# Expert tiles as two 64-row halves in half columns of the array, two tiles per step

## The chip, the cores and the metric

The kernel runs on one core of one Trainium2 chip. The metric is the device time in microseconds (us); lower is better. A core has TensorE for matrix products (PE in the profile, its weight loads PEld), VectorE (DVE), ScalarE (ACT), GpSimd (POOL) and SyncE (SP).
## The reference, cut to what matters

One layer over 4096 tokens of width D = 256: an attention part with fast weights, then a mixture of experts (E = 64 experts, TOP_K = 6 for each token, hidden width F = 176), then a shared expert and a weighted sum.

```python
scores = jax.nn.softmax(x @ gate_w.T, axis=-1)
topk_w, topk_idx = jax.lax.top_k(scores, TOP_K)        # 6 of 64 experts for each token
...
buf = zeros((E, C, D)).at[se, pos_c].add(x[st])         # rows sorted by expert, C = 768 at most
g = jnp.einsum('ecd,efd->ecf', buf, w_gate)
u = jnp.einsum('ecd,efd->ecf', buf, w_up)
eo = jnp.einsum('ecf,edf->ecd', jax.nn.silu(g) * u, w_down)
gathered = eo[se, pos_c] * (sw * valid)[:, None]
y = jnp.zeros_like(x).at[st].add(gathered)
```

There are 4096 x 6 = 24576 (token, expert) rows, 384 for an expert in the mean; how many each expert has is known only on the chip. Everything in the expert stage is float32.

## The kernel before

Five phases follow each other, with all engines meeting between them: `phase_qkv`, `phase_fast_weights` (which also normalises, picks the experts and scatters each row to its expert's stretch of `scratch_buf`), `phase_route`, `phase_experts` and `phase_combine`.

`phase_route` counts the rows of each expert and makes tables for the expert tiles: for tile n the first row in `scratch_buf` (`first_row`), the expert (`need`, as its number plus one), and which of the tile's rows are real (`slot`, `beyond`). A tile is 128 rows of one expert. The number of tiles is fixed when the kernel is built, by the worst case: (24576 + 64 x 127) / 128, rounded up to a multiple of 128, is NT = 256. Meanwhile POOL scatters the last rows (L1603) and SP loads the first four experts.

`phase_experts` runs 256 steps, all unrolled, on every engine in an order written out by hand. For tile n:

- ACT's sequencer loads `first_row[n]` into a register (`load_x`, L1779) and issues the DMA of 128 rows into `xg` (L1781), some six tiles ahead;
- PE turns the tile (`turn_x`, L1721, two 128x128 transposes into `psX`), ACT copies it to `xT` (L1791);
- PE multiplies it with the gate and up weights (`gate_up`, L1735, `psGU`, 352 columns, two products of depth 128). The weights lie in a ring of eight experts; which slot is read from `need[n]` by PE's sequencer (`expert_of`, L1725). ACT makes the silu (`sgm`, L1787), DVE the product (`hh`, L1868);
- PE turns `hh` (`turn_h`, L1743 and L1744, `psH`), DVE copies it to `hT` (L1846);
- PE makes the down product (`down`, L1751, `psD`, 256 columns, two products of depth 88), ACT copies it to `eo` (L1798), POOL scatters the rows to `scratch_y` (L1709) at places that DVE worked out (L1851, L1871).

One step of PE is `gate_up(n-1), turn_x(n), turn_h(n-2), down(n-3)`; one of ACT is silu(n-1), copy of x(n), copy of the output(n-3), `load_x(n+6)`. DVE also makes the tokens' weights in these steps (L1821 to L1862). SP refills the ring as experts are done with (`freed`). `phase_combine` gathers, weighs and adds.

In `phase_fast_weights` there is a product that the later text uses: `token_product` (L764), whose stationary operands are 64 columns wide and whose outputs lie in the upper and the lower 64 partitions of PSUM by turns:

```python
for h in range(H):
    for b2 in range(2):
        mm = pe.matmul(dst[CH * b2:CH * b2 + CH, h * HD:(h + 1) * HD],
                       kvT[:, x, j0 + h, b2, :], src[:, 2 * b2 + h, :], start=True, stop=True)
```

Of the kernel before, what the change touches and what calls it, by code (L numbers as in the profile page):

```python
# [6 lines left out]
F32 = mybir.dt.float32  # L7
# [23 lines left out]
NT = -(-((N * TOPK + E * (P - 1)) // P) // P) * P  # L31
WRING = 8
FIRST = 4
# [1352 lines left out]
def load_expert(sp, T, wgu, wd, ex, buf, done):  # L1386
    FH = F // 2
    for c, key in enumerate(("wgT", "wuT")):
        sp.dma_start(wgu[:, bass.ds(buf, 1), :, c * F:(c + 1) * F].rearrange("p b k n -> p (b k) n"),
                     T[key].rearrange("e (k p) n -> e p k n", p=P)  # L1390
                     [bass.ds(ex, 1), :, :, :].rearrange("e p k n -> (e p) k n")).then_inc(done, 16)
    sp.dma_start(wd[0:FH, bass.ds(buf, 1), :, :].rearrange("p b k n -> p (b k) n"),
                 T["wdT"].rearrange("e (k p) n -> e p k n", p=FH)
                 [bass.ds(ex, 1), :, :, :].rearrange("e p k n -> (e p) k n")).then_inc(done, 16)

def phase_route(nc, T, z, mask, run, ones, low, valid, slot, beyond, need, first_row, freed, wgu, wd, rows, dest):

    TC = NT // P  # L1400
    HP = E // 2
    with ExitStack() as ctx:
# [10 lines left out]
        identb = sb("identb", [P, P], BF16)  # L1413
# [4 lines left out]
        lane = sb("lane", [P, 2])  # L1418
        total = sb("total", [P, E])
        end = sb("end", [P, 2 * E])  # L1420
        ended = sb("ended", [P, 3, TC, E])
        col = sb("col", [P, 4, TC])
        left = sb("left", [P, TC])
        back = sb("back", [P, TC])
        cols = sb("cols", [P, 4 * TC, P], BF16)
        row = sb("row", [P, 3, NT])
# [6 lines left out]
        psT = ctx.enter_context(nc.psum_tensor("t_psT", [P, 2, NT], F32))  # L1433
        psL = ctx.enter_context(nc.psum_tensor("t_psL", [P, 2, NT], F32))
# [8 lines left out]
        def _(v):  # L1443
# [25 lines left out]
            v.wait_ge(s_pool, 9)  # L1469
# [3 lines left out]
            for c in range(TC):  # L1473
# [3 lines left out]
                                            op0=ALU.is_le, op1=ALU.mult, accum_out=col[:, 1, c:c + 1]))  # L1477
# [4 lines left out]
            step(v.tensor_tensor(col[:, 1, :], tcol[:, :], col[:, 1, :], ALU.subtract))  # L1482
            settle()
            step(v.scalar_tensor_tensor(out=left[:, :], in0=col[:, 1, :], scalar=-float(P), in1=left[:, :], op0=ALU.mult, op1=ALU.add))
            settle()
            step(v.tensor_scalar(left[:, :], left[:, :], 0.0, float(P), ALU.max, ALU.min))
            step(v.tensor_scalar(back[:, :], col[:, 1, :], 1.0, None, ALU.min))
            settle()
            step(v.tensor_scalar(col[:, 2, :], left[:, :], -1.0, float(P), ALU.mult, ALU.add))
            settle()  # L1490
            step(v.tensor_tensor(col[:, 2, :], col[:, 2, :], back[:, :], ALU.mult))
            settle()
            step(v.tensor_tensor(col[:, 3, :], col[:, 2, :], left[:, :], ALU.add))
            settle()
            step(v.tensor_copy(cols[:, :, :], col[:, :, :].rearrange("p a c -> p (a c)").unsqueeze(2).broadcast_to([P, 4 * TC, P])), "cols")
            step(v.tensor_scalar(freed[:, WRING:E], end[0:1, 0:E - WRING], float(TILES_AHEAD), None, ALU.add))
# [4 lines left out]
            v.wait_ge(s_row, 1)  # L1501
            step(v.tensor_scalar(row[:, 0, :], psT[:, 0, :], float(STRETCH), None, ALU.mult))
            step(v.tensor_scalar(need[:, :], psT[0:1, 0, :], float(E - 1), 1.0, ALU.min, ALU.add))
            settle()
            step(v.scalar_tensor_tensor(out=row[:, 1, :], in0=psT[:, 1, :], scalar=float(P), in1=row[:, 0, :],
                                        op0=ALU.mult, op1=ALU.add))
            v.wait_ge(s_left, 1)
            settle()
            step(v.tensor_tensor(row[:, 2, :], row[:, 1, :], psL[:, 0, :], ALU.subtract))
            settle()  # L1510
            step(v.tensor_scalar(first_row[:, :], row[0:1, 2, :], float(E * STRETCH), None, ALU.min))
            step(v.tensor_scalar(slot[:, :], row[:, 2, :], float(E * STRETCH), lane[:, 1:2], ALU.min, ALU.add))
# [6 lines left out]
            step(v.tensor_scalar(outside[:, 0, :], psL[:, 0, :], lane[:, 0:1], BIG, ALU.is_gt, ALU.mult))  # L1519
            step(v.tensor_scalar(outside[:, 1, :], psL[:, 1, :], lane[:, 0:1], BIG, ALU.is_le, ALU.mult))  # L1520
# [14 lines left out]
        @block.sync  # L1535
        def _(sp):
            for ex in range(FIRST):
                load_expert(sp, T, wgu, wd, ex, ex, s_w)
            sp.wait_ge(s_w, 48 * FIRST)

        @block.tensor
        def _(pe):
            pe.matmul(psN[0:E, 0:1], run[:, TT, :], ones[:, 0:1], start=True, stop=True)
            pe.matmul(psN[:, P:P + E], ones[:, :], run[:, TT, :], start=True, stop=True).then_inc(s_count, 1)
            pe.wait_ge(s_pool, 9)
# [3 lines left out]
            for a in range(2):  # L1549
                for c in range(TC):  # L1550
                    mm = pe.matmul(psT[:, a, c * P:(c + 1) * P], cols[:, a * TC + c, :], identb[:, :], start=True, stop=True)
            mm.then_inc(s_row, 1)
            for a in range(2):
                for c in range(TC):
                    mm = pe.matmul(psL[:, a, c * P:(c + 1) * P], cols[:, (2 + a) * TC + c, :], identb[:, :], start=True, stop=True)
            mm.then_inc(s_left, 1)
# [13 lines left out]
        def _(pool):  # L1570
# [4 lines left out]
            pool.memset(identb[:, :], 0.0).then_inc(s_pool, 1)  # L1575
            pool.wait_ge(s_pool, 4)
# [4 lines left out]
            pool.affine_select(out=identb[:, :], in_=identb[:, :], compare_op=ALU.not_equal, fill=1.0, base=0,  # L1581
                               pattern=[[-1, P]], channel_multiplier=1).then_inc(s_pool, 1)
            pool.iota(tcol[:, :], pattern=[[P, TC]], base=0, channel_multiplier=1,
# [5 lines left out]
            pool.wait_ge(s_pool, 11)  # L1589
# [18 lines left out]
def phase_experts(nc, T, ident, slot, beyond, need, first_row, freed, p, mask, valid, key, keys, wk, wgu, wd, wsh, wdn, xh):  # L1608
# [5 lines left out]
    TI = 8  # L1614
# [3 lines left out]
    XA = GB - 2  # L1618
    WEIGHTS = 28
    with ExitStack() as ctx:  # L1620
# [20 lines left out]
        picked = sb("picked", [P, 2, E])  # L1641
        psX = ps("psX", [P, 2, 512])
# [15 lines left out]
        def thru(n):  # L1658
            return TILES_AHEAD + 1 + n

        def steps(eng, step, after):

            for n in range(NT + after):
# [461 lines left out]
```

## Time and profile before

| what | value |
|---|---|
| time, median of 3 runs | 1771.67 us (1770.18 to 1774.84) |
| the profiled execution's own time | 1769.68 us |
| its span, first to last instruction | 1767.3 us |
| PE busy over the span | 90% |
| DVE, ACT, POOL busy | 65%, 50%, 46% |
| mean granted TensorE clock | 0.964 of full |
| expert steps, 971 to 1617 us | PE busy 643.61 of 646.00 us |

The profiled execution takes 2.4 us more than its span, and is 2.0 us below the median of the runs. Shares of busy time are means over phases with different limits; the stage that the change touches has to be read by itself. A row of a timeline merges equal instructions (x4) and gives the start of the first and the time to the end of the last. Matrix products are pipelined: one shows from its first input to its last output, so that the next starts well before it ends.

### The profile page before, as it was taken

Reading aid. Unit: us, or ns where it says so; the run is one execution under the profiler, and the core shown is the slowest. Engines: PE = TensorE matmul, PEld = TensorE weight load, DVE = VectorE, ACT = ScalarE, POOL = GpSimd, SP = SyncE. Lnnn points to the kernel's source line nnn. Section 1 sums busy time; section 2 is a strip of 40 time slices with the busy share of each in tenths; the row PEclk is TensorE's granted clock in tenths of the full one; section 3 lists DMA queues with packets and bytes.
Section 4 is the critical chain, followed back from the end, with each engine's and each line's share of the span. In section 5 each row is a group of like instructions: output and inputs, shape, how many; then the busy total and the mean of one; then the engine's idle time right before and its main releaser. Section 6 shows DMA issues by size and latency. Waiting matters only on the chain. (4 is left out here: it accounts for less than half of the span.)

```text
span 1767.3 us, 40874 instructions
## 1 busy us (share of the span) xinstructions
PE 1591.9 (90%) x11235; PEld 1184.7 (67%) x11235; DVE 1147.2 (65%) x4093; ACT 880.9 (50%) x2156; POOL 817.9 (46%) x882
## 2 busy tenths in 40 slices
PE   7995999888889888988862999999999999998997
PEld 4664667666666666666652677777777777776775
DVE  5664878788888788888864554444444444433887
ACT  4773767666666666666641333333333333332221
POOL 2322334566566566666675233333333343343333
PEclk9996999999999999999965999999999999999998
DMA  3864444444444532232224656556555656322996
GB/s 131 258 226 153 129 143 128 156 134 141 152 150 153 163 95 83 83 89 83 74 89 135 183 175 186 172 171 185 171 175 176 182 179 194 98 54 62 252 245 152
DMA packets 260031, 263.27 MB, mean 149 GB/s; under 512 B 83563, under 2 KB 231385, under 8 KB 259824
## 3 DMA queue, kind: packets, MB, share of 16 engines
q1 hardware_dynamic: 196016, 170.45, 33.4%
q0 software_dynamic: 21504, 51.18, 8.2%
q10 hardware_dynamic: 42304, 39.08, 8.1%
q8 instruction: 105, 1.72, 0.4%
q14 instruction: 102, 0.84, 0.2%
HBM read 141.78 MB, written 127.18 MB: 152 GB/s over the span
## 5 line engine op out<-in xcount | busy, mean ns | idle before, releaser
L1709 POOL DMA_INDIRECT scratch_y<-e_eo,e_goes x256 | 251.7, 983 | 405.3 <-ACT e_eo L1798 336.6
L1735 PE MATMUL e_psGU<-wgu,e_xT 128*128 x1024 | 352.1, 466 | 3.1 <-issue 2.3
L1846 DVE COPY e_hT<-e_psH 88x256 f32<-88x256 f32 x256 | 107.7, 421 | 338.6 <-PE e_psH L1744 242.2
L1751 PE MATMUL e_psD<-wd,e_hT 88*128 x1024 | 263.6, 379 | 0.0
L1735 PEld LDWEIGHTS e_psGU<-wgu,e_xT 128*128 128x128 f32 x1024 | 186.7, 190 | 87.6 <-issue 18.3
L1369 POOL TENSOR_TENSOR f_wnr<-f_wss,f_half 128x4 f32<-128x4 f32 x96 | 109.3, 1139 | 230.7 <-DVE f_wss L1192 230.1
L1359 POOL DMA_INDIRECT scratch_buf<-rows,dest x180 | 185.3, 1030 | 45.5 <-issue 43.7
L1787 ACT ACTIVATE e_sgm<-e_psGU 128x176 f32<-128x176 f32 x256 | 81.2, 317 | 238.5 <-PE e_psGU L1735 206.6
L1751 PEld LDWEIGHTS e_psD<-wd,e_hT 88*128 88x128 f32 x1024 | 173.8, 190 | 14.3 <-issue 0.3
L1798 ACT ACTIVATE e_eo<-e_psD 128x256 f32<-128x256 f32 x256 | 98.1, 383 | 161.8 <-issue 87.6
L1721 PEld LDWEIGHTS e_psX<-ident,e_xg 128*128 128x128 f32 x512 | 72.4, 142 | 76.7 <-issue 40.8
L1721 PE MATMUL e_psX<-ident,e_xg 128*128 128x128 f32 x512 | 98.6, 274 | 9.0 <-DMA e_xg<-scratch_buf 9.0
L1011 ACT ACTIVATE f_wsq<-f_WT 128x512 f32<-128x512 f32 x96 | 60.6, 631 | 74.3 <-DVE f_WT L1188 68.9
L1791 ACT ACTIVATE e_xT<-e_psX 128x256 f32<-128x256 f32 x256 | 97.2, 380 | 0.4
L856 PEld LDWEIGHTS prod<-f_A 128*128 128x128 bf16 x768 | 59.8, 99 | 46.6 <-issue 2.2
L979 ACT ACTIVATE f_X<-spare 128x512 bf16<-128x512 f32 x96 | 57.4, 598 | 65.8 <-PE spare L873 65.8
L284 PE MATMUL q_psQ<-q_wq,q_hT 128*128 128x512 f32 (+1 forms) x256 | 90.2, 496 | 0.0
L1868 DVE TENSOR_TENSOR e_hh<-e_psGU,e_sgm 128x176 f32<-128x176 f32 x256 | 84.9, 332 | 3.6 <-ACT e_sgm L1787 3.6
L2025 DVE SCALAR_TENSOR_TENSOR c_acc<-c_g,wk,c_acc 128x256 f32<-128x256 f32 x160 | 78.6, 491 | 5.7
L853 PE MATMUL prod<-f_gamma_r,f_gamma_l 128*128 128x512 bf16 x192 | 74.7, 389 | 7.0 <-DVE f_A L1179 6.4
L856 PE MATMUL prod<-f_A 128*128 128x128 bf16 x768 | 75.1, 221 | 0.0
L979 ACT ACTIVATE f_B<-prod 128x512 bf16<-128x512 f32 x96 | 57.0, 595 | 35.6 <-PE prod L856 22.6
(303 smaller groups left out, 3773.2 us busy)
## 6 DMA issues: line engine op xcount, KB each, us to landing
e_xg<-scratch_buf ACTq DMA_DIRECT2D x256, 132.0 KB
scratch_y<-f_blank SPq DMA_DIRECT2D x64, 384.0 KB
c_g<-scratch_y SPq DMA_DIRECT2D x64, 384.0 KB, 6.1
scratch_qkvT<-q_tT SPq DMA_DIRECT2D x16, 768.0 KB, 5.1
wgu<-in_wgT SPq DMA_DIRECT2D x64, 176.0 KB
wgu<-in_wuT SPq DMA_DIRECT2D x64, 176.0 KB
wd<-in_wdT SPq DMA_DIRECT2D x64, 176.0 KB
scratch_buf<-f_blank SPq DMA_DIRECT2D x65, 132.0 KB, 1.9
```

Source lines behind the costliest of these rows:

```text
L284: mm = pe.matmul(psQ[:, u, lo:hi], hT[:, b % 2, k, u, :], wq[:, k, lo:hi], start=(k == 0), stop=(k == KD - 1))
L856: mm = pe.matmul(dst[:, q, :], a[:, x, m, q, :], a[:, x, m, q, :], start=False, stop=(q == Q - 1))
L979: act.activation(dst, src, ACT.Copy, scale=scale).then_inc(done.sem, 1)
L1359: pool.indirect_dma_start(out=T["buf"], out_offset=bass.IndirectOffsetOnAxis(dest[:, i, k:k + 1], 0), in_=rows[:, i % RR, :], in_offset=No ...
L1369: pool.tensor_tensor(wnr[:, x, cols], wss[:, x, cols], half[:, 0:Q], ALU.pow).then_inc(wn1[x].sem, 1)
L1709: pool.indirect_dma_start(out=T["y"], out_offset=bass.IndirectOffsetOnAxis(goes[:, n:n + 1], 0), in_=eo[:, n % OB, :], in_offset=None, bou ...
L1721: mm = pe.transpose(psX[:, j % 2, k * P:(k + 1) * P], xg[j % GB][:, k * P:(k + 1) * P], ident[:, :])
L1735: mm = pe.matmul(psGU[:, j % 2, 0:2 * F], xT[:, j % 2, k, :], wgu[:, bass.ds(buf, 1), k, :].rearrange("p b n -> p (b n)"), start=(k == 0), ...
L1751: mm = pe.matmul(psD[:, j % 2, 0:D], hT[0:FH, j % 2, k, :], wd[0:FH, buf, k, :].rearrange("p b n -> p (b n)"), start=(k == 0), stop=(k == 1))
L1791: act.activation(xT[:, j % 2, :, :].rearrange("p k t -> p (k t)"), psX[:, j % 2, 0:KD * P], ACT.Copy).then_inc(xd, 1)
L1798: act.activation(eo[:, b % OB, :], psD[:, b % 2, 0:D], ACT.Copy).then_inc(eod, 1)
L1846: v.tensor_copy(hT[0:FH, b, :, :].rearrange("p k t -> p (k t)"), psH[0:FH, b, 0:2 * P]).then_inc(htd, 1)
```

## The change

An expert tile becomes two halves of 64 rows, each with a first row and an expert of its own (mostly the same one, at a border two). NT becomes (24576 + 64 x 63) / 64, halved and rounded up to a multiple of 8: 224. The two halves share the tile's 128 partitions. `turn_x` and `turn_h` stay whole; the products of `gate_up` and `down` are split into one of 64 stationary columns for each half, side by side in the array: the first half reads its weights from the ring at an address known only at run time, the second from a copy, `up2` and `down2`, that ACT (`keep_up`, 128x704) and DVE (`keep_down`, 88x512) make for each tile. `load_x` issues two DMAs of 64 rows. Every engine works on two tiles in a step, and the register values of two tiles (four entries of a table) are loaded by one call, `numbers`, without a check of bounds. POOL waits for an expert's weights (`has_come`, one register load for each tile) and tells ACT. `phase_route` makes tables of half tiles: other small DVE work, seven smaller products in place of eight for the tables (their number of columns is much the same), one identity less on POOL.

```diff
-NT = -(-((N * TOPK + E * (P - 1)) // P) // P) * P
+RT = P // 2
+NT = -(-((N * TOPK + E * (RT - 1)) // RT) // 16) * 8
...
+        def numbers(engine, table, lo, hi, n):
+            _, values = nc.values_load_multi_w_load_instructions(
+                table[0:1, 2 * n:2 * n + 4], [engine], min_val=lo, max_val=hi, skip_runtime_bounds_check_because=IN_RANGE)
+            return {n + i // 2: values[i // 2 * 2:i // 2 * 2 + 2] for i in (0, 2)}
...
         def _(pool):
+            def has_come(m):
+                pool.wait_ge(ready, pool.value_load(need[0:1, 2 * m + 1:2 * m + 2], min_val=1, max_val=E))
+                pool.sem_inc(present, 1)
...
         def _(pe):
+            def find(n):
+                for m, (e1, _) in numbers(mybir.EngineType.PE, need, 1, E, n).items():
+                    at[m] = pe.snap((e1 + (NB - 1)) % NB * WROW)
-            def gate_up(n, j, expert):
-                e1, buf = expert
-                pe.wait_ge(ready, e1)
+            def gate_up(n):
+                pe.wait_ge(up_kept, n + 1)
                 pe.wait_ge(xd, thru(n))
                 pe.wait_ge(hd, thru(n - 2))
                 for k in range(KD):
-                    mm = pe.matmul(psGU[:, j % 2, 0:2 * F], xT[:, j % 2, k, :],
-                                   wgu[:, bass.ds(buf, 1), k, :].rearrange("p b n -> p (b n)"),
+                    pe.matmul(psGU[0:RT, n % 2, 0:2 * F], xT[:, n % 2, k, 0:RT], ring[:, bass.ds(at[n] + k * 2 * F, 2 * F)],
+                              start=(k == 0), stop=(k == KD - 1))
+                    mm = pe.matmul(psGU[RT:P, n % 2, 0:2 * F], xT[:, n % 2, k, RT:P], up2[:, n % 2, k * 2 * F:(k + 1) * 2 * F],
                                    start=(k == 0), stop=(k == KD - 1))
...
+                pe.wait_ge(down_kept, n + 1)
                 for k in range(2):
+                    pe.matmul(psD[0:RT, n % 2, 0:D], hT[0:FH, n % 2, k, 0:RT], ring[0:FH, bass.ds(at[n] + UP + k * D, D)],
+                              start=(k == 0), stop=(k == 1))
+                    mm = pe.matmul(psD[RT:P, n % 2, 0:D], hT[0:FH, n % 2, k, RT:P], down2[:, n % 2, k * D:(k + 1) * D],
+                                   start=(k == 0), stop=(k == 1))
...
+            for n in range(-2, NT + 2, 2):
+                each(gate_up, n)
+                each(down, n - 2)
+                each(turn_x, n + 2)
+                if 0 <= n + 2 < NT:
+                    find(n + 2)
+                each(turn_h, n)
...
         def _(act):
+            def load_x(m):
+                if m >= GB:
+                    act.wait_ge(xp, thru(m - GB))
+                    act.wait_ge(goes_d, m - GB + 1)
+                act.sem_inc(a_carrier, 1)
+                for h, at in enumerate(rows.pop(m)):
+                    act.dma_start(xg[m % GB][h * RT:(h + 1) * RT, :], T["buf"][bass.ds(at, RT), :]).then_inc(gi[m % GB], 16)
+            def keep_up(n):
+                e1 = experts.pop(n)[1]
+                act.wait_ge(present, n + 1)
+                act.wait_ge(gup, thru(n - 2))
+                act.sem_inc(a_carrier, 1)
+                act.activation(up2[:, n % 2, :], ring[:, bass.ds((e1 + (NB - 1)) % NB * WROW, UP)], ACT.Copy).then_inc(up_kept, 1)
...
+            for n in (0, 2):
+                find_rows(n)
+                load_x(n)
+                load_x(n + 1)
+            act.preload_act_table_set("silu_and_others")
+            find_experts(0)
+            keep_up(0)
+            keep_up(1)
+            for n in range(-2, NT + 2, 2):
+                (find_rows(n + 6), find_experts(n + 2), silu(n), keep_up(n + 2), load_x(n + 6), silu(n + 1),
+                 keep_up(n + 3), keep_out(n - 2), load_x(n + 7), keep_x(n + 2), keep_x(n + 3), keep_out(n - 1))
...
         def _(v):
+            def keep_down(n):
+                v.wait_ge(up_kept, n + 1)
+                v.wait_ge(dp, thru(n - 2))
+                at = (experts.pop(n)[1] + (NB - 1)) % NB * WROW + UP
+                v.tensor_copy(down2[:, n % 2, :], ring[0:FH, bass.ds(at, 2 * D)]).then_inc(down_kept, 1)
+            for n in range(0, NT + 2, 2):
+                (keep_h(n - 2), keep_h(n - 1), own(n), weigh(n), own(n + 1), weigh(n + 1), hidden(n), leave(n),
+                 hidden(n + 1), leave(n + 1), numbers(DVE, need, n), keep_down(n), keep_down(n + 1))
```

The loops of ACT and DVE are written here in one line each, without the conditions for the first and the last tiles. `find_rows` and `find_experts` are `numbers` on `first_row` and `need`. `keep_x`, `keep_out`, `keep_h`, `own`, `hidden`, `leave` are the old work on L1791, L1798, L1846, L1851, L1868 and L1871 under names.

## Rows read from the trace of the kernel before

**Rows 1.** The page: busy us, share of the span and instructions of each engine.

```profile
PE 1591.9 (90%) x11235; PEld 1184.7 (67%) x11235; DVE 1147.2 (65%) x4093; ACT 880.9 (50%) x2156; POOL 817.9 (46%) x882
```

**Rows 2.** Windows: end of route, expert steps, drain, combine.

```profile
930.00:971.00 41.00, 10.23 (x56) 7.07 (x56) 20.16 (x98) 5.75 (x7) 23.41 (x39) 0.54 0.41 131
971.00:1617.00 646.00, 643.61 (x3054) 478.21 (x3055) 305.22 (x1677) 248.62 (x763) 247.75 (x252) 0.99 0.54 159
1617.00:1627.00 10.00, 5.24 (x21) 3.23 (x19) 1.42 (x6) 1.47 (x4) 3.94 (x4) 0.90 0.05 8
```

**Rows 3.** Timeline of one steady expert step: start, us, engine, line, idle before.

```profile
1613.47 1.35 PE L1735 MATMUL e_psGU<-wgu,e_xT 128*128 x4
1614.66 0.38 PE L1721 MATMUL e_psX<-ident,e_xg 128*128 128x128 f32 x2
1614.86 0.32 ACT L1787 ACTIVATE e_sgm<-e_psGU 128x176 f32<-128x176 f32 x1 [0.80 <-PE e_psGU L1735]
1614.88 0.27 PE L1743 MATMUL e_psH<-ident,e_hh 128*88 128x128 f32 x1
1615.09 1.03 PE L1751 MATMUL e_psD<-wd,e_hT 88*128 x4
1615.96 1.35 PE L1735 MATMUL e_psGU<-wgu,e_xT 128*128 x4
```

**Rows 4.** Timeline of ACT alone over one step of the expert stage.

```profile
1303.90 0.32 ACT L1787 ACTIVATE e_sgm<-e_psGU 128x176 f32<-128x176 f32 x1 [0.85 <-PE e_psGU L1735]
1304.11 0.38 ACT L1791 ACTIVATE e_xT<-e_psX 128x256 f32<-128x256 f32 x1
1305.18 0.38 ACT L1798 ACTIVATE e_eo<-e_psD 128x256 f32<-128x256 f32 x1 [0.69 <-issue]
1306.24 0.36 ACTq L1781 DMA_DIRECT2D e_xg<-scratch_buf  x1
1306.64 0.32 ACT L1787 ACTIVATE e_sgm<-e_psGU 128x176 f32<-128x176 f32 x1 [1.08 <-PE e_psGU L1735]
```

**Rows 5.** Timeline of PE around one `token_product` (L764).

```profile
408.38 0.66 PE L901 MATMUL prod<-ident,f_WT 128*128 128x128 f32 x4 [0.77 <-DVE f_WT L1205]
408.96 0.66 PE L764 MATMUL prod<-f_Wn,f_kvT 128*64 128x128 f32 x8
409.55 0.66 PE L964 MATMUL spare<-wgate,f_h2T 128*128 128x64 f32 x4
```

**Rows 6.** Lines L1779 and L1781, 1100 to 1500 us: ns, min/median/max.

```profile
L1779 ACTq TENSOR_LOAD <-first_row x159: 276/349/566, 1100.7 to 1498.2; - x159
L1779 ACTq FUSED_REGOPS  x159: 152/152/158, 1101.2 to 1498.5; - x159
L1781 ACTq FUSED_REGOPS  x159: 42/42/42, 1101.5 to 1498.8; - x159
L1781 ACTq MOVE e_xg<-scratch_buf x159: 29/29/38, 1101.6 to 1498.9; - x159
L1781 ACTq DMA_DIRECT2D e_xg<-scratch_buf x159: 353/358/430, 1101.6 to 1499.2; - x159
```

**Rows 7.** Groups of instructions with 512 columns, as the nearest to the new copies.

```profile
L1011 ACT ACTIVATE f_wsq<-f_WT x96: 621/630/664, 177.2 to 896.0; 128x512 f32<-128x512 f32 x96
L1188 DVE TENSOR_TENSOR f_WT<-prod,f_WT 128x512 f32<-128x512 f32 x3 | 2.1, 689 | 2.2 <-PE prod L890 2.2
```

**Rows 8.** Timeline where the expert steps begin.

```profile
967.32 1.54 ACTq L1781 DMA_DIRECT2D e_xg<-scratch_buf  x2
970.29 0.38 ACT L1791 ACTIVATE e_xT<-e_psX 128x256 f32<-128x256 f32 x1
970.95 2.71 PE L1735 MATMUL e_psGU<-wgu,e_xT 128*128 x4 [0.70 <-ACT e_xT L1791]
978.57 2.11 PE L1735 MATMUL e_psGU<-wgu,e_xT 128*128 x4 [0.24 <-issue]
```

**Rows 9.** Timeline of the last scatter and of the combine's first product.

```profile
1622.37 0.98 POOL L1709 DMA_INDIRECT scratch_y<-e_eo,e_goes  x1 [0.30 <-issue]
1625.60 2.69 PE L1950 MATMUL c_psG<-wsh,xh 128*128 128x352 f32 x4 [4.72 <-PEq L67]
```

**Rows 10.** Route: POOL's group of scatters, and the last work of DVE.

```profile
L1603 POOL DMA_INDIRECT scratch_buf<-rows,dest x12 | 11.9, 988 | 3.5 <-issue 3.5
963.77 1.45 DVE L1525 TENSOR_SCALAR valid<-t_psV 128x512 bf16<-128x512 f32 x2 [4.28 <-DMA f_qT<-scratch_qkvT]
```

More of the change, by code:

```diff
@@ L29 @@
 TT = N // P
-NT = -(-((N * TOPK + E * (P - 1)) // P) // P) * P
+RT = P // 2
+NT = -(-((N * TOPK + E * (RT - 1)) // RT) // 16) * 8
 WRING = 8
+UP = 2 * F * KD
+WROW = UP + 2 * D
+IN_RANGE = "route clips the table's entries to these bounds"
 FIRST = 4
@@ L1500, in _ @@
                 settle()
[L1501 to L1512, printed above, removed]
             for g in range(NG):
@@ L1617, in phase_experts @@
     OB = 4
-    XA = GB - 2
+    SEEN = 6
     WEIGHTS = 28
@@ L1753, in down @@
                 mm.then_inc(dp, 1)
-            def step(n, j):
-                if real(n, 1):
-                    up = expert_of(n - 1)
-                    gate_up(n - 1, (j - 1) % TI, up)
-                if real(n, 3):
-                    out_of = expert_of(n - 3)
-                if real(n, 0):
-                    turn_x(n, j)
-                if real(n, 2):
-                    turn_h(n - 2, (j - 2) % TI)
-                if real(n, 3):
-                    down(n - 3, (j - 3) % TI, out_of)
@@ L1768, in _, with each @@
-            steps(pe, step, 3)
+                del at[n]
+            def each(stage, n):
+                for m in (n, n + 1):
+                    if 0 <= m < NT:
+                        stage(m)
+            for n in range(-2, NT + 2, 2):
[5 more added lines that the diff above has]
+                each(turn_h, n)
         @block.scalar
@@ L1773, in _, with silu, keep_x, keep_out @@
                 act.sem_inc(s, TILES_AHEAD)
+            def silu(n):
+                act.wait_ge(gup, thru(n))
+                act.activation(sgm[:, n % 2, :], psGU[:, n % 2, 0:F], ACT.Silu).then_inc(sgd, 1)
+            def keep_x(n):
+                act.wait_ge(xp, thru(n))
+                act.wait_ge(gup, thru(n - 2))
+                act.activation(xT[:, n % 2, :, :].rearrange("p k t -> p (k t)"), psX[:, n % 2, 0:KD * P],
+                               ACT.Copy).then_inc(xd, 1)
+            def keep_out(n):
+                act.wait_ge(dp, thru(n))
+                if n >= OB:
+                    act.wait_ge(out[n % OB], n // OB * 16)
+                act.activation(eo[:, n % OB, :], psD[:, n % 2, 0:D], ACT.Copy).then_inc(eod, 1)
+            rows, experts = {}, {}
+            def find_rows(n):
+                rows.update(numbers(mybir.EngineType.Activation, first_row, 0, E * STRETCH, n))
+            def find_experts(n):
+                experts.update(numbers(mybir.EngineType.Activation, need, 1, E, n))
             def load_x(m):
@@ new lines, in _ @@
+            for n in (0, 2):
[7 more added lines that the diff above has]
+            for n in range(-2, NT + 2, 2):
+                if real(n, -6):
+                    find_rows(n + 6)
+                if 2 <= n + 2 < NT:
+                    find_experts(n + 2)
+                if real(n, 0):
+                    silu(n)
+                    if real(n, -2):
+                        keep_up(n + 2)
+                if real(n, -6):
+                    load_x(n + 6)
+                if real(n, 0):
+                    silu(n + 1)
+                    if real(n, -2):
+                        keep_up(n + 3)
+                if real(n, 2):
+                    keep_out(n - 2)
+                if real(n, -6):
+                    load_x(n + 7)
+                if real(n, -2):
+                    keep_x(n + 2)
+                    keep_x(n + 3)
+                if real(n, 2):
+                    keep_out(n - 1)
```

257 lines of the change are left out of this document (136 added, 121 removed).

## The prediction

> **What bounds the kernel now.** I read the page's busy shares first: PE leads with 90%, but that is a mean over five phases [rows 1]. So I cut the span into windows by phase. In the expert steps PE is busy 643.61 of 646.00 us, DVE 305 us, ACT 249 us, POOL 248 us [rows 2]: the stage is bound by PE alone, and the others have 1.3 to 1.5 us free in each step. One steady step of the timeline says what PE does in it: from one `gate_up` to the next are 1615.96 - 1613.47 = 2.49 us [rows 3]. Of these `gate_up` takes 1.19 (to the start of `turn_x`), `turn_x` and `turn_h` 0.43 together, `down` 0.87 (1615.09 to 1615.96). There is no gap, so a step is the sum of what PE streams, and ACT, whose silu starts 0.03 to 0.05 us after `gate_up` ends, is on no path as long as it keeps up.
>
> The whole stage: the first `gate_up` starts at 970.95 [rows 8], the last, 255 steps later, at 1615.96 [rows 3]: 645.0 us, 2.529 a step. 255 steps of 2.487 would be 634.2; of the other 10.8 about 2.7 are the start, where two steps take 7.62 us at a low clock [rows 8], and 8.1, or 0.032 a step, are steps in which something is late. Rows 4 show what: a register load and a DMA issue end just when the silu starts (1306.24 + 0.36 = 1306.60, silu at 1306.64). ACT's sequencer is close behind PE.
>
> **What goes: 32 of 256 steps.** The rest of the change decides what a step costs. If it cost nothing, 32 x 2.52 = 81 us would go.
>
> **PE's products.** There are as many columns to stream as before, if the two halves run side by side, and twice as many if not. The trace has such products: `token_product` makes four float32 products of 64 stationary columns, 128 moving, in alternating halves, as eight records. In the full array a record of 128 columns takes 0.107 (`gate_up`: 1.19 / 4 = 0.298 for 352 columns, so 0.108 for 128). Eight would take 0.86, but the next line starts 0.59 after L764 [rows 5]: they run in pairs, 4 x 0.107 = 0.43. What is left over is the price of going in and out of half columns: the last record of L901 starts at 408.38 + 0.66 - 0.27 = 408.77, L964 at 409.55; 0.78 less its own 0.107 and less 0.43 is 0.24 us. An iteration of two tiles goes in and out once. So PE needs 2 x 2.487 + 0.24 = 5.21 us for two tiles, 2.61 a step. Bounds: 2.49 (the price of the switch vanishes) and, with no pairing at all, 2 x (1.19 + 0.87) + 0.43 + 0.12 = 4.67; I take the pairing, for the row is the same kind of product, only narrower.
>
> **PE's register loads** fall from two a step to one for two tiles, and before they hid behind queued products; I count nothing. If that cover goes, one load of 0.35 and its arithmetic of 0.15 stand in the open in an iteration, 0.25 a step.
>
> **ACT.** New are `keep_up` (704 columns; 512 take 0.630 [rows 7], 176 take 0.32 and 256 take 0.38 [rows 4], so 0.83 ns a column and 0.79 us), a second DMA for each tile (0.358 + 0.042 + 0.029 = 0.43 us of its sequencer [rows 6]) and loads of four values in place of one. I lay this out with T = 0 where `gate_up(n)` starts. silu(n) starts at T+1.4, `keep_up(n+2)` runs to 2.45, hiding one pair of DMA issues; silu(n+1) waits for PE until 2.57, `keep_up(n+3)` runs to 3.65, the output copy to 4.0, two DMA issues to 4.5. PE's `turn_x(n+2)` is done at 2.38 + 1.74 + 0.12 + 0.22 + 0.17 = 4.63, so the copy of x runs 4.65 to 5.03, and `gate_up(n+2)` could start at 5.07 where PE comes to it at 5.21. Then ACT copies x(n+3) and output(n-1), and its sequencer is free at about 5.4. The next silu is due at 5.21 + 1.4 = 6.6. In between stand `find_rows` and `find_experts`: 1.2 us of room, and with 0.15 of slack at the silus and 0.15 at the copy of x, 1.5 us. They cost two loads and some 0.3 of address arithmetic. If a load of four values takes what a load of one takes, 0.349 and 0.152 [rows 6], it is 1.3 us: it fits, barely. No row shows a load of several values: its bounds are 0.35 and four times that, 1.4. I take the low end, since it is one call with neighbouring values and the check that costs arithmetic today is gone; the high end is a rival.
>
> **DVE** is busy 1.19 a step [rows 2]; `keep_down` adds at most 0.69 [rows 7] and a load 0.25, so 2.1 of 2.61: hidden. Its copy of `hT(n)` comes behind both `keep_down`, at about T+5.9, and `down(n)` wants it at 5.21 + 2.4 = 7.6. **POOL**: 0.98 for a scatter and about 0.55 for `has_come`, 1.5 of 2.61; hidden. If the weights of a tile six ahead were late, POOL would hold back scatters and ACT `keep_up`; SP refills eight experts ahead, so I count nothing.
>
> **The ends.** Before, the first DMA issue is at 967.32 and the first copy of x at 970.29 [rows 8]. Now twelve DMA issues (5.2 us), four register loads (1.6) and part of two `keep_up` (1.6) stand before that copy: about 8 us instead of 3, +5. Filling and draining in pairs: +1 each; before, the last scatter starts 6.4 us after the last `gate_up`, and combine's first product 3.2 us later [rows 9]. Together +7, between +3 and +11. In route POOL's twelve scatters, 0.99 each with 0.3 between [rows 10], and not the tables, fill the time; they can start 0.5 earlier, DVE has some more small steps: 0, give or take 1.5.
>
> **Sum.** From the first to the last `gate_up`: 223 x (2.605 + 0.032) + 2.7 = 590.8 against 645.0: -54.2. With the ends -47.2. The profiled execution's own time, 1769.68, becomes 1722.5; the median of the runs is 2.0 above it: 1724.5.
>
> **The rivals.** *ACT is late because of its register loads; it decides from 0.81 us a load* (slower). The excess over PE's iteration is 2 x load + 0.3 - 1.5. The gain is used up when a step takes (645.0 - 7 - 2.7) / 223 - 0.032 = 2.817, an iteration 5.63, an excess of 0.42, a load of 0.81. At four times 0.349 = 1.4 the excess is 1.6: 5.21 + 1.6 = 6.8, 3.4 a step, 223 x 3.44 + 2.7 = 770, so about 1769.7 + 125 + 7 + 2 = 1904. For it speaks that ACT has only 0.2 us to spare; against it that all four values lie side by side. Chance 0.19.
>
> *The same in between*: a load of 0.70, the geometric middle of the bounds, gives an excess of 0.2, a step of 2.71, 223 x 2.74 + 2.7 = 613.7: -31 + 7, so about 1747. Chance 0.17, with 0.06 more for a time within 0.3% of before. The Trainium skill (Runtime: NRT & Kernel Launch, Instruction fetch mechanics) says that register loads cost about 200 ns for each register, in bulk too. By an estimate from that page four registers are 0.8 us, the excess 0.4, and the time would be about that of before. This trace has 0.35 us for one register; no row has several.
>
> *The halves don't pair* at 352 columns or with an address known only at run time: 4.67 a step, 223 x 4.7 = 1048, some 2180 us. Rows 5 speak against it; chance 0.03. That the switch costs nothing, with ends of +3, gives 223 x 2.52 + 2.7 = 564.7, -80 + 3: 1695; chance 0.05.
>
> **Numbers.** The forecast itself, 1700 to 1742, has 0.50; its own range takes loads up to 0.6 us, ends of +3 to +11, a switch of 0.1 to 0.3. Adding the middle rival and the slower one up to about 1 us a load gives 1700 to 1805 for 8 in 10. Faster 0.72, same 0.06, slower 0.22; 0.3% of the time, 5.3 us, is about what a measurement tells from no change.
>
> **What would show it.** In the profile after: 224 tiles; `gate_up` records in pairs, an iteration near 5.2 us; about 0.1 us of PE idle before the first half product and before `turn_x`; `up2` copies of 0.79 us; a four-value load of 0.35 to 0.4 us on ACTq. If PE waits for ACT's copy of x and ACT's silu starts later than 0.05 us after `gate_up` ends, with register loads ahead of it, the rival has it. The first copy of x should come about 5 us later than before. I am wrong if PE's busy time in the stage falls while its span doesn't, or if pairs are absent.

## The result, and the profile after

The changed kernel takes 1788.2 us (median of 4 runs, 1781.58 to 1794.65) against 1770.93 for the kernel before (4 runs, 1767.56 to 1774.84): ratio 1.0092, 95% interval 1.0064 to 1.0121. It is 0.9% slower, where 1724.5 us was forecast. The profiled execution, the fastest of the four, took 1781.58 us, its span is 1779.7.

The page's busy shares answer to [rows 1], the window of the expert steps to [rows 2]:

```profile
PE 1549.5 (87%) x12655; PEld 1056.7 (59%) x12655; DVE 1219.9 (69%) x4177; ACT 999.9 (56%) x2284; POOL 788.9 (44%) x848
```

```profile
976.00:1622.00 646.00, 592.79 (x4424) 345.53 (x4424) 372.02 (x1731) 365.53 (x888) 217.47 (x219) 1.00 0.52 151
```

PE was busy 643.61 of 646.00 us in the expert steps; now it is busy 592.79 of 646.00. It does 51 us less work in the same time: the saving is there, and has turned into 53 us of idle. The page's groups say in front of what it waits:

```profile
L1769 PE MATMUL e_psGU<-wexp,e_xT 128*64 x896 | 290.2, 467 | 57.7 <-issue 52.5
L1771 PE MATMUL e_psGU<-e_up,e_xT 128*64 128x352 f32 x896 | 290.7, 468 | 0.0
```

Behind the first bar stand the busy time (us) and the mean of one (ns), behind the second PE's idle time before them. It is all in front of `gate_up`'s first half product. "issue" names nobody, so one iteration (two tiles) has to be read. The timeline from one `gate_up` of a pair to the next, PE, ACT and ACT's queue; columns as in [rows 3]:

```profile
1341.05 0.32 ACT L1813 ACTIVATE e_sgm<-e_psGU 128x176 f32<-128x176 f32 x1 [1.15 <-PE e_psGU L1771]
1341.29 0.79 ACT L1848 ACTIVATE e_up<-wexp 128x704 f32 x1
...
1341.53 1.14 ACTq L1841 DMA_DIRECT2D e_xg<-scratch_buf  x2
...
1341.72 0.46 PE L1769 MATMUL e_psGU<-wexp,e_xT 128*64 x1
...
1341.73 0.46 PE L1771 MATMUL e_psGU<-e_up,e_xT 128*64 128x352 f32 x1
...
1342.72 0.32 ACT L1813 ACTIVATE e_sgm<-e_psGU 128x176 f32<-128x176 f32 x1 [0.64 <-PE e_psGU L1771]
...
1342.98 0.79 ACT L1848 ACTIVATE e_up<-wexp 128x704 f32 x1
...
1343.32 0.49 ACTq L1841 DMA_DIRECT2D e_xg<-scratch_buf  x1
...
1343.54 0.38 PE L1788 MATMUL e_psD<-e_down,e_hT 88*64 88x256 f32 x1
...
1343.85 0.66 PE L1761 MATMUL e_psX<-ident,e_xg 128*128 128x128 f32 x4
1343.96 0.49 ACTq L1841 DMA_DIRECT2D e_xg<-scratch_buf  x1
...
1344.56 0.66 ACT L1818 ACTIVATE e_xT<-e_psX 128x256 f32<-128x256 f32 x2 [0.51 <-PE e_psX L1761]
...
1345.20 0.51 PE L1769 MATMUL e_psGU<-wexp,e_xT 128*64 x1 [0.26 <-issue]
```

Read it backwards. `gate_up` starts at 1345.20, 0.26 us after the first copy of x has ended (1344.56 + 0.38; the row's 0.66 is that of two copies). That copy starts right behind the second DMA issue of a pair (1343.96 + 0.49 = 1344.45), not behind `turn_x`. This pair is late because silu(n+1) started at 1342.72 and not at 1342.25, when its products had ended (1341.73 + 0.46 is 1342.19); what ended just before it is the other pair of issues (1341.53 + 1.14 = 1342.67). The same kernel, 40 us earlier, where one issue takes 0.91:

```profile
1301.79 0.91 ACTq L1841 DMA_DIRECT2D e_xg<-scratch_buf  x1
1302.15 0.37 ACT L1825 ACTIVATE e_eo<-e_psD 128x256 f32<-128x256 f32 x1
1302.86 0.50 ACTq L1841 DMA_DIRECT2D e_xg<-scratch_buf  x1
1303.46 0.66 ACT L1818 ACTIVATE e_xT<-e_psX 128x256 f32<-128x256 f32 x2 [0.94 <-PE e_psX L1761]
...
1304.10 0.51 PE L1769 MATMUL e_psGU<-wexp,e_xT 128*64 x1 [0.69 <-issue]
```

Here the copy of x is held up by 0.4 us more, and the gap in front of `gate_up` is 0.69 in place of 0.26: what ACT's queue holds ahead of that copy reaches PE in full. The source rows, 1100 to 1500 us, price the steps of ACT and DVE (ns, min/median/max, as [rows 6]):

```profile
L1687 ACTq TENSOR_LOAD <-first_row x68: 305/309/322, 1105.2 to 1495.7; - x68
L1687 ACTq TENSOR_LOAD <-need x68: 304/306/325, 1105.5 to 1496.0; - x68
...
L1841 ACTq DMA_DIRECT2D e_xg<-scratch_buf x274: 480/491/1278, 1101.2 to 1498.7; - x137
...
L1848 ACT ACTIVATE e_up<-wexp x138: 789/790/792, 1100.9 to 1499.5; 128x704 f32 x138
...
L1955 DVE COPY e_down<-wexp x136: 415/423/425, 1103.5 to 1495.1; 88x512 f32 x136
```

The four-value load, which decided between forecast and slower rival, is 0.31 us, cheaper than the load of one value before. The DMA issue, taken from [rows 6] as 0.358, is 0.491: it moves 64 rows now and not 128. Of all 448 issues 41 take over 0.56 us (these I call long); none of the 256 before took over 0.43. They do not come just anywhere: 31 are the second of a pair, 10 the third issue of an iteration, 0.65 us behind the first pair; the first of an iteration, 2.7 us behind the one before it, is never long.

From the start of the first `gate_up` (976.68) to that of the last iteration (1622.07) are 645.4 us, 111 iterations of 5.814. The median iteration, from the starts of `gate_up` in the trace, is 5.62; a quarter take more than 5.97. The 38 iterations with a long issue in them take 6.10 in the mean, the other 73 take 5.67.

The ends. Where the expert steps begin and where they end (answers to [rows 8] and [rows 9]):

```profile
966.44 5.57 ACTq L1841 DMA_DIRECT2D e_xg<-scratch_buf  x8
...
976.68 0.84 PE L1769 MATMUL e_psGU<-wexp,e_xT 128*64 x1 [5.14 <-ACT e_xT L1818]
```

```profile
1633.46 0.98 POOL L1743 DMA_INDIRECT scratch_y<-e_eo,e_goes  x1 [2.55 <-issue]
```

The first `gate_up` comes 5.7 us later than before. The last tile's `gate_up` is at 1623.30, combine's first product at 1636.70, 13.4 us later; before it was 9.6. The span adds up: last tile's `gate_up` minus first 646.6 against 645.0 (+1.6), start +5.7, drain +3.8, after that +1.3: 12.4 us, which is 1779.7 - 1767.3.

### The profile page after: what moved, and what is told of

Same layout as the page of the kernel before. It is cut to its first block and busy times, and to the rows that moved or that the text cites. A ratio compares the mean times of both kernels' runs of the same rounds, so it can differ in the third digit from the quotient of the medians.

```text
span 1779.7 us, 43893 instructions
## 1 busy us (share of the span) xinstructions
PE 1549.5 (87%) x12655; PEld 1056.7 (59%) x12655; DVE 1219.9 (69%) x4177; ACT 999.9 (56%) x2284; POOL 788.9 (44%) x848
## 5 line engine op out<-in xcount | busy, mean ns | idle before, releaser
L1769 PE MATMUL e_psGU<-wexp,e_xT 128*64 x896 | 290.2, 467 | 57.7 <-issue 52.5
L1771 PE MATMUL e_psGU<-e_up,e_xT 128*64 128x352 f32 x896 | 290.7, 468 | 0.0
L1769 PEld LDWEIGHTS e_psGU<-wexp,e_xT 128*64 128x64 f32 x896 | 114.0, 137 | 185.9 <-issue 87.9
L1786 PE MATMUL e_psD<-wexp,e_hT 88*64 x896 | 211.9, 379 | 0.6 <-DVE e_hT L1917 0.6
L1788 PE MATMUL e_psD<-e_down,e_hT 88*64 88x256 f32 x896 | 211.9, 379 | 0.0
L1848 ACT ACTIVATE e_up<-wexp 128x704 f32 x224 | 176.9, 790 | 0.2 <-issue 0.2
L1786 PEld LDWEIGHTS e_psD<-wexp,e_hT 88*64 88x64 f32 x896 | 122.2, 136 | 79.3 <-issue 0.9
L1788 PEld LDWEIGHTS e_psD<-e_down,e_hT 88*64 88x64 f32 x896 | 122.2, 136 | 0.0
L1771 PEld LDWEIGHTS e_psGU<-e_up,e_xT 128*64 128x64 f32 x896 | 114.0, 137 | 0.0
L1955 DVE COPY e_down<-wexp 88x512 f32 x224 | 93.0, 423 | 22.9 <-PE e_psD L1788 2.5
```

The source lines that it names most:

```text
L1769: pe.matmul(psGU[0:RT, n % 2, 0:2 * F], xT[:, n % 2, k, 0:RT], ring[:, bass.ds(at[n] + k * 2 * F, 2 * F)], start=(k == 0), stop=(k == KD - 1))
L1771: mm = pe.matmul(psGU[RT:P, n % 2, 0:2 * F], xT[:, n % 2, k, RT:P], up2[:, n % 2, k * 2 * F:(k + 1) * 2 * F], start=(k == 0), stop=(k == K ...
L1786: pe.matmul(psD[0:RT, n % 2, 0:D], hT[0:FH, n % 2, k, 0:RT], ring[0:FH, bass.ds(at[n] + UP + k * D, D)], start=(k == 0), stop=(k == 1))
L1788: mm = pe.matmul(psD[RT:P, n % 2, 0:D], hT[0:FH, n % 2, k, RT:P], down2[:, n % 2, k * D:(k + 1) * D], start=(k == 0), stop=(k == 1))
L1848: act.activation(up2[:, n % 2, :], ring[:, bass.ds((e1 + (NB - 1)) % NB * WROW, UP)], ACT.Copy).then_inc(up_kept, 1)
L1955: v.tensor_copy(down2[:, n % 2, :], ring[0:FH, bass.ds(at, 2 * D)]).then_inc(down_kept, 1)
```

## The experiments

Kernel n below is that of experiment n; what the expectations call e1 to e6 are kernels 1 to 6. An iteration is two tiles. The theories, as the expectations name them: **A**, ACT is late for its copy of x because of what its queue holds (issues, copies of weights); **B**, PE itself pays, for the half columns; **C**, DVE is late; **D**, the long issues come at random and cannot be arranged away. The experiments ran on three chips, on which the kernel before takes 1732.48, 1782.35 and 1733.44 us, so a time is compared only with kernels on its own chip; between chips I compare iterations (first to last start of `gate_up` over 111, and the median). If nothing changes, an iteration is the changed kernel's: 5.81 in the mean, 5.62 in the median.

**1. The copy of 704 columns and its load go from ACT to DVE.**

```diff
-            def keep_up(n):                      # ACT
-                act.activation(up2[:, n % 2, :], ring[...], ACT.Copy).then_inc(up_kept, 1)
+            def keep_up(n):                      # DVE
+                v.tensor_copy(up2[:, n % 2, :], ring[...]).then_inc(up_kept, 1)
```

> The 128x704 copies of the up weights and their register load move from ACT to DVE; results unchanged. Theory A (ACT is the late engine: its DMA issues of 0.49 us and its copies of 0.79 us stand before silu and before the copy of x that gate_up waits for): an iteration of two tiles falls from 5.81 to about 5.3 us, the time to 1730 to 1745 us, some 50 us under the changed kernel and 30 under the one before. Theory B (half columns, run-time addresses and PE's own waits make the iteration 5.6 to 5.8): no change, 1780 to 1795. Theory C (DVE becomes the late engine, 2.2 us of 2.6 a tile): above 1790.

1731.43 us (10 runs) against 1732.48 for before (13 runs): ratio 0.9996 (0.9986 to 1.0005). The iteration is 5.71, median 5.59. Taking 1.6 us of copies and a load from ACT gives only 0.1 us back; the 5.3 of theory A is missed. 36 issues are long, up to 1.73 us. If ACT is late, it is not mainly for its copies. DVE has 1.03 us more to do in an iteration and nothing gets slower, so C is out.

**2. After the first eight tiles only one DMA for each tile** (the other 64 rows are old ones and are not scattered).

```diff
-                for h, at in enumerate(rows.pop(m)):
+                for h, at in enumerate(rows.pop(m)[0:2 if m < GB else 1]):
```

> Only the first 64 rows of each tile are loaded (after the first eight tiles); the second half keeps old rows and is not scattered: one DMA issue for each tile in place of two, all else as in the changed kernel. Theory A: 2 x 0.56 us less of ACT's sequencer in an iteration, which falls to 5.3 to 5.4 us, the time to about 1740. Theory B: 5.8 us, 1780 or more. If ACT's copies alone make it late and not the issues: 5.7.

1695.75 us (one run), 36.7 less than before on that chip; iteration 5.370, median 5.36. All work of PE, both copies and all loads are still there; every second issue is gone, with the rows that it would bring and their scatter (kernel 5 has these back at the same median, so that traffic is not what counts). ACT's timeline:

```profile
1302.82 0.32 ACT L1814 ACTIVATE e_sgm<-e_psGU 128x176 f32<-128x176 f32 x1 [1.15 <-PE e_psGU L1772]
1303.07 0.79 ACT L1849 ACTIVATE e_up<-wexp 128x704 f32 x1
1303.32 0.48 ACTq L1842 DMA_DIRECT2D e_xg<-scratch_buf  x1
1304.01 0.32 ACT L1814 ACTIVATE e_sgm<-e_psGU 128x176 f32<-128x176 f32 x1
...
1305.10 0.49 ACTq L1842 DMA_DIRECT2D e_xg<-scratch_buf  x1
1306.10 0.66 ACT L1819 ACTIVATE e_xT<-e_psX 128x256 f32<-128x256 f32 x2 [0.78 <-PE e_psX L1762]
```

silu(n+1) is 1.19 us behind silu(n), as PE's products are, where it was 1.67 behind; the copy of x has 0.5 us of free queue ahead of it. And the long issues are gone, though no issue became shorter as such (source rows, 1000 to 1550 us):

```profile
L1842 ACTq DMA_DIRECT2D e_xg<-scratch_buf x197: 481/490/519, 999.7 to 1524.8; - x197
```

**3. ACT's copy cut to 8 of 704 columns** (the second halves use fixed weights), both issues kept.

```diff
-                act.activation(up2[:, n % 2, :], ring[:, bass.ds(..., UP)], ACT.Copy).then_inc(up_kept, 1)
+                act.activation(up2[:, n % 2, 0:8], ring[:, bass.ds(..., 8)], ACT.Copy).then_inc(up_kept, 1)
```

> ACT's copy of the up weights is cut to 128x8 (both buffers are filled once before; the second half computes with those weights), the two DMA issues and all loads and waits stay. Theory A: the copies hide the first pair of issues, so that without them the issues alone are left: silu(n+1) some 0.3 us late in place of 0.5, an iteration of about 5.4 us, 1745. If the issues alone matter: 5.8. Theory B: 5.8.

1751.17 us (one run); 5.821, median 5.63: no change. The copies of 0.79 us are hidden behind the issues (A had them share the blame, and 5.4 expected). In this kernel's timeline, in an iteration with a long issue, the copy of x sits right behind a pair of 1.43 us:

```profile
1305.19 1.43 ACTq L1842 DMA_DIRECT2D e_xg<-scratch_buf  x2
1306.73 0.66 ACT L1819 ACTIVATE e_xT<-e_psX 128x256 f32<-128x256 f32 x2 [1.40 <-PE e_psX L1762]
```

**4. The kernel before, with two DMAs of 64 rows for each tile** and nothing else of the change.

```diff
-                act.dma_start(xg[m % GB][:, :], T["buf"][bass.ds(at, P), :]).then_inc(gi[m % GB], 16)
+                for h in range(2):
+                    act.dma_start(xg[m % GB][h * CH:(h + 1) * CH, :], T["buf"][bass.ds(at + h * CH, CH), :]).then_inc(gi[m % GB], 16)
```

> The kernel before, with each tile of 128 rows loaded by two DMAs of 64 rows; results unchanged. It prices the second issue alone. If a 64-row issue takes 0.49 us as in the changed kernel, ACT's sequencer needs 1.12 us in place of 0.43 where it has no room: a step goes from 2.53 to about 3.1 us, the time to 1890 to 1930. If it takes 0.36, as the prediction had it: 2.9 us, about 1870. Theory B: no change, 1771.

1823.6 us (one run) against 1732.48: 91 us more, 2.871 a step where it was 2.529. Two issues, 1.17 us where one was 0.36, end right before a silu, which PE is then waiting for:

```profile
1302.61 1.17 ACTq L1782 DMA_DIRECT2D e_xg<-scratch_buf  x2
1303.82 0.32 ACT L1788 ACTIVATE e_sgm<-e_psGU 128x176 f32<-128x176 f32 x1 [1.60 <-PE e_psX L1721]
```

The direction is A's, the size six tenths of what was expected (0.34 us a step for 0.57): of 0.8 us more in the queue 0.34 reach PE. It also shows that halves cost 0.48 each without anything else of the change (source rows, 1000 to 1550 us):

```profile
L1782 ACTq DMA_DIRECT2D e_xg<-scratch_buf x386: 479/484/1239, 1000.0 to 1548.4; - x193
```

**5 and 6. The four issues of an iteration one by one**, before silu(n), before silu(n+1), before the output copy and before the copy of x; with the copy of 704 columns on DVE (5) and on ACT (6). **7.** The changed kernel once more on that chip.

```diff
-                if real(n, -6):
-                    load_x(n + 6)
+                if ahead:
+                    load_half(n + 6, 1)
                 if real(n, 0):
                     silu(n + 1)
...
+                if ahead:
+                    load_half(n + 7, 0)
                 if real(n, 2):
                     keep_out(n - 2)
-                if real(n, -6):
-                    load_x(n + 7)
+                if ahead:
+                    load_half(n + 7, 1)
```

> As e1 (copies of the up weights on DVE), and on ACT the four DMA issues of an iteration are spread one by one: before silu(n), before silu(n+1), before the output copy, before the copies of x. Theory A, sharpened by the first four runs (what counts is which 0.49 us issues stand back to back before silu(n+1) and before the copy of x; the copies don't count): an iteration of about 5.4 us with hardly any scatter, against 5.71 in e1 and 5.81 in the changed kernel; a ratio of 0.98 to the kernel before. Rival D (an issue is sometimes long, 0.8 to 1.3 us, whatever stands around it, and the mean comes from those): the usual iteration falls to 5.4, but the mean stays above 5.6, a ratio of 0.99 to 1.0.

> The changed kernel with the four DMA issues spread alone, the copies left on ACT. Both register loads and an issue then stand between the last output copy and silu(n), 1.4 us in 1.5 us of room. Theory A: 5.4 to 5.6 us an iteration, a ratio to the kernel before of 0.98 to 1.0. If the order doesn't matter: 5.8 and 1.009 as the changed kernel.

> The changed kernel itself, on the chip of these runs, to be compared with them and with the kernel before. Both theories: a ratio to the kernel before near 1.009, 5.8 us an iteration.

| kernel | time, us (runs) | ratio to before (95%) | iteration: mean, median |
|---|---|---|---|
| before | 1782.35 (10) | | |
| changed | 1796.6 (7) | 1.0086 (1.0058 to 1.0114) | 5.822, 5.61 |
| 5: spread, copy on DVE | 1751.69 (4) | 0.9814 (0.9766 to 0.9861) | 5.405, 5.36 |
| 6: spread, copy on ACT | 1759.44 (4) | 0.9875 (0.9831 to 0.9918) | 5.534, 5.46 |

Kernel 5 issues as many DMAs as the changed one and computes the same, and is 45 us faster than it; 0.417 an iteration over 111 iterations is 46. It beats the kernel before by 1.9% (1.4 to 2.3). ACT's timeline:

```profile
1299.26 0.32 ACT L1813 ACTIVATE e_sgm<-e_psGU 128x176 f32<-128x176 f32 x1 [1.15 <-PE e_psGU L1771]
1299.48 0.48 ACTq L1837 DMA_DIRECT2D e_xg<-scratch_buf  x1
1300.44 0.32 ACT L1813 ACTIVATE e_sgm<-e_psGU 128x176 f32<-128x176 f32 x1 [0.87 <-PE e_psGU L1771]
1300.67 0.49 ACTq L1837 DMA_DIRECT2D e_xg<-scratch_buf  x1
1301.31 0.38 ACT L1825 ACTIVATE e_eo<-e_psD 128x256 f32<-128x256 f32 x1 [0.55 <-DVE e_goes L1936]
1301.54 0.48 ACTq L1837 DMA_DIRECT2D e_xg<-scratch_buf  x1
1302.54 0.66 ACT L1818 ACTIVATE e_xT<-e_psX 128x256 f32<-128x256 f32 x2 [0.84 <-PE e_psX L1761]
```

No two issues touch, and only 15 of 448 are long, where the changed kernel has 41 and kernel 1, in pairs, 36. So D does not hold: spreading removes most of them, and they do not come at random. In all traces with issues of 64 rows the longest pause before a long issue is 1.09 us (kernel 6); of 1433 issues with more than 1.15 us of pause before them none is long. Closeness alone is not all of it either: in kernel 4 only 11 of 251 second ones of a pair are long, in the changed kernel 31 of 224. Kernel 6 says that the two copies and their register load on ACT matter once the pairs are gone: 0.13 us an iteration; which of the two it is was not told apart. Nine iterations of kernel 5 are over 5.45: the first, 6.65, is the start of the stage (6.65 in kernel 2 as well), seven have a long issue of 0.77 to 1.45 us in them, and one of 6.36 stays open.

The traces also say where the time is lost. Medians over the iterations but the first and last five, from the starts of the instructions, in us:

| kernel | `gate_up` to `turn_x` | `turn_x` to first copy of x (mean) | end of the copy to `gate_up` | silu(n+1) behind silu(n) |
|---|---|---|---|---|
| changed | 4.25 | 0.73 (0.93) | 0.26 | 1.67 |
| 1 | 4.25 | 0.71 (0.82) | 0.26 | 1.40 |
| 2 | 4.25 | 0.47 (0.47) | 0.26 | 1.18 |
| 3 | 4.25 | 0.74 (0.94) | 0.26 | 1.67 |
| 5 | 4.25 | 0.47 (0.50) | 0.26 | 1.18 |

Only the stretch from `turn_x` to the copy differs: 4.25 + 0.47 + 0.38 + 0.26 is 5.36, and with 0.93 in place of 0.47 it is 5.82. Kernel 1 adds that the late silu(n+1) is not needed for it: there it is only 0.2 late, and the pair of issues behind the output copy is enough to hold the copy of x back by 0.24.

**8. Three more four-value loads in each iteration of ACT.**

> The changed kernel with three more register loads of four values (0.31 us each) ahead of find_rows on ACT: 0.93 us more between the last output copy and silu(n). Theory A gives that stretch about 0.5 us of room: the iteration grows by about 0.4 to 0.5 us, the time by 45 to 55 us. If register loads stand in the open, as in the slower rival of the prediction: 0.93 us, 105 us. If ACT's sequencer has room everywhere (theory B): nothing.

1792.74 us, 5.838. It says nothing of loads: the profile has as many L1687 loads on ACT as that of the changed kernel, 112 of each table, so the added ones, whose values nobody uses, did not run. It is one more run of the changed kernel, whose three traces have 5.814, 5.822 and 5.838.

**9. ACT's values loaded one by one**, six loads an iteration in place of two.

```diff
-                rows.update(numbers(mybir.EngineType.Activation, first_row, 0, E * STRETCH, n))
+                for m in (n, n + 1):
+                    rows[m] = [one(first_row, 0, E * STRETCH, 2 * m + h) for h in range(2)]
```

> The changed kernel with ACT's register values loaded one by one: six loads of about 0.31 us in an iteration in place of two, 1.24 us more between the last output copy and silu(n). It puts the slower rival of the prediction to the test. In the changed kernel the two loads end 1.25 us before silu(n) starts, so by theory A (the issues alone are what is late) the iteration hardly grows, 0 to 0.15 us from 5.82. If loads stand in the open as that rival had it: up to 1.24 us more, 7.0.

1759.22 us against 1733.44 (one run each); 5.912, median 5.85. Source rows, 1100 to 1500 us:

```profile
L1830 ACTq TENSOR_LOAD <-first_row x268: 272/280/467, 1102.8 to 1496.0; - x134
L1830 ACTq TENSOR_LOAD <-need x134: 272/278/716, 1104.1 to 1496.6; - x134
```

Six of 0.28 in place of two of 0.31 are 1.06 us more on ACT's queue; they cost 0.09 in the mean and 0.23 in the median (there are fewer long issues, 30). silu(n), which starts 1.45 us behind `gate_up` in the changed kernel as in kernel 2, starts 1.59 behind it here: the room ahead of it is just used up. Had the loads stood in the open already, as the slower rival had it, nearly all of the 1.06 would have come through. That rival falls.

**10. Kernel 5 with full products of 128 columns** (both halves with the first half's weights; copies, loads and issues kept).

```diff
-                    pe.matmul(psGU[0:RT, ...], xT[:, n % 2, k, 0:RT], ring[...], ...)
-                    mm = pe.matmul(psGU[RT:P, ...], xT[:, n % 2, k, RT:P], up2[...], ...)
+                    mm = pe.matmul(psGU[:, ...], xT[:, n % 2, k, :], ring[...], ...)
```

> As e5, with each pair of half products replaced by one product of 128 stationary columns with the weights of the first half's expert (rows of a second expert get wrong weights); copies, loads, waits and order stay. It prices the half columns on PE: in e5 the usual iteration is 5.36 us. If pairs run fully side by side and only the switches cost, about 0.1 on the path before turn_x and some of that before gate_up: 5.2 to 5.3. If the halves cost more than the switches (imperfect pairs): below 5.15. If nothing: 5.36.

1687.61 us against 1733.44 (one run each); 5.287, median 5.253. Against kernel 5's 5.359 the half columns cost 0.106 an iteration, 12 us in all: B is real and small (0.06 of it before `turn_x`, which comes at 4.19 for 4.25, and 0.05 between `turn_x` and the copy, 0.42 for 0.47). The rest of kernel 10's excess over 2 x 2.487 = 4.97 is not the half columns. PE's timeline shows where most of it is:

```profile
1300.67 1.89 PE L1784 MATMUL e_psD<-wexp,e_hT 88*128 x8
1302.39 0.60 PE L1761 MATMUL e_psX<-ident,e_xg 128*128 128x128 f32 x4
...
1303.16 0.27 PE L1777 MATMUL e_psH<-ident,e_hh 128*88 128x128 f32 x1
1303.45 1.74 PE L1769 MATMUL e_psGU<-wexp,e_xT 128*128 x5
```

`turn_x` to `gate_up` is 1.06 us, for 0.88 of PE's work. The chain beside it is `turn_x` to copy of x 0.43 (ACT at 1302.82), the copy 0.38, and 0.25 from its end to the product.

## Why the prediction was wrong, step by step

**The step that failed** is the layout of ACT: "a second DMA for each tile (0.358 + 0.042 + 0.029 = 0.43 us of its sequencer [rows 6])", "hiding one pair of DMA issues", and from it "`gate_up(n+2)` could start at 5.07 where PE comes to it at 5.21". Three terms in it:

1. *Copy of x to `gate_up`.* I took 0.04 us; it is 0.26 in the changed kernel and 0.25 in kernel 10. [Rows 8] had it: the copy ends at 970.67, `gate_up` starts at 970.95. With it, and 0.48 from `turn_x` to the copy (1305.62 to 1306.10 in kernel 2) where I had 0.41, `gate_up` can't come before about 5.35; kernel 2's median is 5.36. So 5.21 became 5.36: 0.15 x 111 = 17 us. Before, `turn_x` lay a whole `down` ahead of its `gate_up` and the latency was covered [rows 3]; the new order puts only `turn_h` between them. That nothing but the order did this is argued: no run has the old order.
2. *The issues.* One of 64 rows takes 0.49, not the 0.36 of one of 128 rows. A pair was to run under a copy of 0.79 us and takes 1.14, starting 0.24 after it: silu(n+1) 0.47 late, the second pair late behind it, the copy of x 0.23 late. Shown by kernel 2 (issues halved: 5.36), kernel 3 (copies gone, issues kept: 5.63) and kernel 5 (issues spread: 5.36). 5.36 to 5.62: 0.26 x 111 = 29 us.
3. *Long issues.* From the median of 5.62 to the mean of 5.81 are 21 us, where I had carried over 10 for late steps and the start (0.032 a step and 2.7): +11. Most of it goes with the long issues: the 38 iterations that have one lift the mean by 0.15, 16 us, over the 5.67 of the others. Kernels 2 and 5, where they are absent or few, have means within 0.05 of their medians.

Together some 57, against a stage 55.8 us longer than forecast (646.6 against 590.8); the count by iterations leaves out the last tile, whose `gate_up` follows its partner's by 1.23 where I had a step of 2.64. The ends were off by 2.5: start +5.7 for +5 and one of filling, drain +3.8 for +1. Together with 1.3 behind combine's first product that is the profile's difference. Of the 17.3 us between the medians the profiled executions show 11.9; the remainder is the spread of the runs.

The sign that I had named did come up: PE's busy time in the stage fell by 51 us and the stage's span did not. The time, 1788.2, does lie in the wide range of 1700 to 1805, but by luck: that range reached so far only for a dear register load, and the load is cheap.

**What held.** The two halves run side by side: L1769 and L1771 start 0.01 us apart, and a pair takes 0.295 as one full product did. That they might not (0.03) is out. The Trainium skill (TensorEngine Tiling (Array Packing), Key Properties) says that a change of tiling mode drains the array. This trace fits it: there is 0.10 us of gap between the last `down` product (1343.54 + 0.215, the time that 256 columns take from one start to the next) and `turn_x` (1343.85), and kernel 10, all in full columns, has none there (1300.67 + 8 x 0.215 = 1302.39). Kernel 10 prices the whole at 0.106 an iteration. Forecast was 0.24: too much, and by luck it made up for part of the missing latency. The copy is 0.79 as forecast. DVE and POOL are hidden (372 and 217 us of 646 busy, and kernel 1's load on DVE costs nothing). The four-value load is 0.31, below my low end. The Trainium skill (Runtime: NRT & Kernel Launch, Instruction fetch mechanics) has about 200 ns for each register, in bulk too. It says so of registers loaded from HBM; the tables here lie in SBUF, so the 0.8 that I worked out from it was for another kind of load, and the measurement decides. So both rivals built on loads are out, although the time came out on their side: the price that would use up the gain, an iteration of 5.63, was exceeded because of another instruction of the same queue, and of the latency.

**What I passed over.** The margin at the copy of x was 0.14 us by my own layout, and none of the prices that it rests on (the issues, the way from `turn_x` to the copy and from the copy to `gate_up`) had bounds; of ACT's prices I gave two bounds only to the load, which stands elsewhere. The DMA of half the rows was as unseen as the load of four values, and got the full-size row's price without a bound; the row of `gate_up`'s first start with its copy was among my own rows and not used for the latency.

**Open.** Why an issue of 64 rows takes 0.13 us longer than one of 128; why some that follow within about a microsecond of another take 0.6 to 1.7 us, and why more of them do in the changed kernel than in kernel 4; one long iteration in kernel 5. SP's issues are not the cause of most: beside 27 of the changed kernel's 41 long ones no DMA issue of SP runs.

## What to carry to other kernels

Lay out an engine's queue with every instruction that it issues, and give each price that no row of the same shape shows, a DMA issue of another size as well, its two bounds; a margin of 0.1 us is no margin. Where a reordering brings a producer next to its consumer, put the whole latency from the end of the copy to the start of the product on the path (0.26 us here). When a queue must issue more transfers, put them one at a time into the gaps between waits: here that alone took 37 us from the changed kernel (kernel 6).

## What the hardware showed unexpectedly

- A DMA issue of 64 rows holds ACT's queue 0.48 to 0.49 us, one of 128 rows 0.358 [rows 6].
- Issues close behind another are sometimes long: 41 of 448 over 0.56 us in pairs (up to 1.28; 1.73 in kernel 1), 11 of 512 in kernel 4, 15 of 448 when spread (kernel 5), none of 232 in kernel 2, and none of 1433 in any trace with more than 1.15 us of pause before it.
- One load instruction brings four neighbouring values in 0.31 us, less than the 0.349 of the single one before [rows 6]; the single ones of kernel 9, without the check of bounds, take 0.28.
- A DVE copy of 88x512 takes 0.423 us, one of 128x704 0.517; ACT takes 0.790 for the latter.
